# A Mamba layer with an MLP on one core: the two branches of TensorE in the MLP with their bodies swapped

## What is computed

```python
x = x + mixer(layernorm(x))
g = (layernorm(x) @ gate_w.T) * gate_s        # gate_w, up_w: (1408, 512)
u = (layernorm(x) @ up_w.T) * up_s
x = x + ((silu(g) * u) @ down_w.T) * down_s   # down_w: (512, 1408)
```

## Time and profile before

| | us |
|---|---|
| median of 3 runs | 828.86 (828.42 to 829.15) |
| profiled execution | 825.1 |
| its span, first to last instruction | 823.0 |
| TensorE busy | 748.8 (91%) |
| VectorE busy | 512.5 (62%) |
| ScalarE busy | 505.9 (61%) |
| GpSimd busy | 298.0 (36%) |

### The profile page before, as it was taken

One profiled execution on the slowest core, in us unless ns is written; L12 is line 12 of the kernel. 1 busy time (PEld: TensorE's weight loads), 2 busy tenths in 40 slices (PEclk: granted clock), 3 DMA queues, 4 the chain that ended last, 5 costly groups with the idle time before them and its releaser, 6 DMA issues. The chain is left out here.

```text
span 823.0 us, 20282 instructions
## 1 busy us (share of the span) xinstructions
PE 748.8 (91%) x8464; PEld 615.0 (75%) x8464; DVE 512.5 (62%) x839; ACT 505.9 (61%) x963; POOL 298.0 (36%) x245
## 2 busy tenths in 40 slices
PE   5874999999999999999999997548989999999997
PEld 4864778788788788878888884436767887887886
DVE  6883976976976976976976966654622632542331
ACT  6984978978978978888888887024511321331330
POOL 2233366375275276276186175021001001002002
PEclk9986999999999999999999999868999999999999
DMA  9705054443443524423523425921003002102102
GB/s 298 214 2 154 12 117 117 78 112 107 94 98 104 126 66 113 129 68 104 136 66 96 117 66 159 401 59 47 26 16 124 17 5 93 56 0 74 28 1 77
DMA packets 39195, 77.67 MB, mean 94 GB/s; under 512 B 9408, under 2 KB 15040, under 8 KB 39104
## 3 DMA queue, kind: packets, MB, share of 16 engines
q1 hardware_dynamic: 38784, 75.84, 33.4%
q10 hardware_dynamic: 320, 0.52, 0.3%
HBM read 67.43 MB, written 8.92 MB: 93 GB/s over the span
## 5 line engine op out<-in xcount | busy, mean ns | idle before, releaser
L409 POOL TENSOR_TENSOR ring<-tokd,ring 128x1024 f32<-128x1024 f32 x64 | 121.9, 1918 | 198.0 <-ACT tokd L574 127.5
L1064 PE MATMUL ps_proj<-xn_hi,win_hi 128*128 128x256 f32 x608 | 179.2, 295 | 13.9 <-ACT dt_v L506 11.3
L1065 PE MATMUL ps_proj<-xn_lo,win_hi 128*128 128x256 f32 x608 | 172.8, 284 | 0.0
L1066 PE MATMUL ps_proj<-xn_hi,win_lo 128*128 128x256 f32 x608 | 172.4, 284 | 0.0
L1064 PEld LDWEIGHTS ps_proj<-xn_hi,win_hi 128*128 128x128 f32 x608 | 116.7, 192 | 28.2 <-issue 12.9
L1065 PEld LDWEIGHTS ps_proj<-xn_lo,win_hi 128*128 128x128 f32 x608 | 116.9, 192 | 0.3
L1066 PEld LDWEIGHTS ps_proj<-xn_hi,win_lo 128*128 128x128 f32 x608 | 116.8, 192 | 0.0
L799 DVE SCALAR_TENSOR_TENSOR cx<-cin,consts,cx 128x256 f32<-128x256 f32 x240 | 96.3, 477 | 0.0
L1367 POOL TENSOR_TENSOR res<-res,hidden 128x512 f32<-128x512 f32 x16 | 20.5, 1282 | 188.4 <-DVE hidden L1442 188.4
L1399 ACT ACTIVATE silu_g<-pb,scales 128x512 f32<-128x512 f32 x44 | 30.3, 688 | 94.4 <-PE pb L1511 94.3
L1511 PE MATMUL pb<-x1n_hi,wg_hi 128*128 128x512 f32 x176 | 70.4, 400 | 13.0 <-issue 13.0
(11 more groups left out here) (148 smaller groups left out, 1502.9 us busy)
## 6 DMA issues: line engine op xcount, KB each, us to landing
ring<-cum_dram SPq DMA_DIRECT2D x128, 256.0 KB, 4.9
xin<-x SPq DMA_DIRECT2D x8, 512.0 KB, 3.9
res<-x SPq DMA_DIRECT2D x32, 128.0 KB, 2.6
x_in_sb<-x_dram SPq DMA_DIRECT2D x4, 1024.0 KB, 5.8
res<-x_dram SPq DMA_DIRECT2D x16, 256.0 KB, 2.7
out<-res SPq DMA_DIRECT2D x16, 256.0 KB, 2.0
x_dram<-res SPq DMA_DIRECT2D x28, 128.0 KB, 2.4
wg<-gate_w SPq DMA_DIRECT2D x4, 704.0 KB, 9.8
```

What stands on the lines that cost most here:

```text
L409: pool.tensor_tensor(ring[:, g, :, :], own, ring[:, g, :, :], ALU.subtract).then_inc(diffed, 1)
L1064: pe.matmul(out, win_hi[:, k, cols], xn_hi[:, k, :], start=(k == 0), stop=False)
L1065: pe.matmul(out, win_hi[:, k, cols], xn_lo[:, k, :], start=False, stop=False)
L1066: made = pe.matmul(out, win_lo[:, k, cols], xn_hi[:, k, :], start=False, stop=(k == KT - 1))
```

## The change

The two tests are turned from "not zero" to "zero", and the bodies change places. What is executed stays the same matmul for matmul. What changes is which body stands first in TensorE's stream, and so which one is reached without a jump and which one ends in a jump over the other.

```diff
             pe.wait_ge(filled, 1)
             pe.wait_ge(hand.low_any_made, 1)
-            with pe.If(pe.value_load(hand.low_any[:, 0:1].bitcast(I32)) != 0):
+            with pe.If(pe.value_load(hand.low_any[:, 0:1].bitcast(I32)) == 0):
+                gate_up(0, True, True)
+            with pe.Else():
                 gate_up(0, False, True)
-            with pe.Else():
-                gate_up(0, True, True)
             pe.wait_ge(hand.low_any_made, 2)
             pe.wait_ge(down_hi_made, MT)
 
-            with pe.If(pe.value_load(hand.low_any[:, 1:2].bitcast(I32)) != 0):
+            with pe.If(pe.value_load(hand.low_any[:, 1:2].bitcast(I32)) == 0):
+                rest(True)
+            with pe.Else():
                 rest(False)
-            with pe.Else():
-                rest(True)
```

## The result

| | before | changed |
|---|---|---|
| median of the runs beside the prediction, us | 828.64 (4 runs, 825.87 to 829.15) | 816.25 (4 runs, 815.75 to 817.18) |
| profiled execution, us | 825.1 | 815.93 |
| its span, us | 823.0 | 813.8 |
| median of all executions recorded, us | 826.57 (69, 822.24 to 831.07) | 816.41 (19, 814.60 to 819.28) |

The changed kernel is faster by 1.4%, ratio 0.9859 with a 95% interval of 0.9835 to 0.9882. Three later comparisons gave 0.9865 [0.9845, 0.9886], 0.9887 [0.9856, 0.9918] and 0.9887 [0.9866, 0.9908]. In us the four differences of medians are 12.4, 10.4, 9.4 and 9.8. The profiled execution fell by 9.2 us, where I had 9.0. How both can be so is the question of the second half of the experiments.

A forecast was written before the change was run, and what follows sets the result against it. TensorE, busy for 91% of the span, was taken to bound the kernel. The terms 4.0 - 0.3 + 3.4 + 1.9 = 9.0 us gave 816.1 us profiled and a median of 819.8 us, range 818.4 to 823.5.

The forecast's parts named there:

- The stalls are loads of code, and falling through avoids them: Both Ifs: compares of 4125 and 3861 ns wait for code not on the chip; falling through takes near 0.1 us.
- the rival in which the compare costs its four microseconds either way: Both Ifs: the compare stays slow even when falling through, so no difference, 828.9 to 829.2 us; chance 0.06.
- the slower case: End of first body: compares stay slow and the jump waits for the array too, 4.2 us later, 833.1 us; chance 0.04.
- First product: First branch: the first gate and up product starts at 554.3 instead of 558.36, a gain of 4.0 us.
- Slow stretch given back, 0.3 us: After the first branch: TensorE's low clock grant may last longer, costing 0 to 0.6 us extra, taken as 0.3.
- The jump is a full load and hidden by the sequencer's lead: End of first body: the jump loads code for 3.86 to 4.13 us while the array works; gain 3.4 us.
- The rule on taken branches: Skill's rule: taken branches outside two fetched pages load; alone it means the exposed-jump rival, 825.5 us, chance 0.07.
- Clock behind the second branch, 1.9 us: First two down products: 11.86 us against 9.98 in later blocks; with the idling gone, the whole 1.9 us is gained.
- The last jump and the loop cost nothing: Kernel end and loop: a 4.1 us jump hidden by array queue and store, the moved loop stays kept; cost nothing.
- From the profile to the median: Last step: the profile's 9.0 us difference taken off the median of before, 828.86 - 9.0 = 819.8 us.

The follow-up runs named there:

- the cut bodies: Kernel before, its order kept, with the first branch's never executed full-precision body cut to 4 or 7 of 11 tiles: 822.35 and 831.07 us, one execution each.
- a_third: The changed kernel again, unchanged, for a third trace and more timed runs: 816.25 us median (4 runs) beside 825.61 of before.
- a_p4: The changed kernel again, unchanged, for a fourth trace and more timed runs: 817.29 us median (6 runs) beside 827.11 of before.

## Right and wrong, step by step

- *The stalls are loads of code, and falling through avoids them.* Right: 98 and 63 ns for the compares, and the cut bodies show that a taken branch is cheap too when it moves no piece (0.46 us against 4.63). The compares that fall through cost 0.1 us, which refutes the rival in which the compare costs its four microseconds either way, and with it the slower case.
- *First product.* I had it 0.8 us behind the value load's start (554.3 against 553.5); it came after 0.8 (554.57 against 553.8). Gain 4.0 us as forecast, counted from the value load.
- *Slow stretch given back, 0.3 us.* None in this trace (42.60 us against 42.61), 0.3 to 0.4 in the other three of the changed kernel. Right in size.
- *The jump is a full load and hidden by the sequencer's lead.* Right, and shown by exposing it. I charged 3.9 to 4.1 us and in the profile it took 3.35, so it ended before VectorE had low_any, and the array waited 0.03 us, not 0.4. That made the gain 3.8 us, not 3.4. Of the other three traces of the changed kernel one agrees (3.29 and 0.04 us), and in two the jump took 3.7 us and the array waited 0.2 us (a_third, a_p4): the lead of 4.3 us just about covers it.
- *The rule on taken branches.* The jump itself cost 3352 ns, with a piece moved beside it, but the time was not lost, since the array had work queued. The first half is what the Trainium skill states (Runtime: NRT & Kernel Launch, Instruction fetch mechanics: a taken branch to a target outside the fetched pages stalls until that page is loaded), and this trace agrees.
- *Clock behind the second branch, 1.9 us.* 11.86 - 10.22 = 1.6 us in this pair of traces. I had taken the whole difference to later blocks (9.98), and 0.2 us of it isn't the clock's: the changed kernel has the full grant there and still takes 10.22, and without branches it is 10.02. In one of the seven traces of before it is worth 2.9.
- *The last jump and the loop cost nothing.* Right: the jump of 3889 ns ended at 808.9, before the array was done (the drain behind it, 314 ns, ended at 809.2), and the pieces of the loop keep their 40.78 us.
- *From the profile to the median: wrong.* The sum was 4.0 - 0.3 + 3.4 + 1.9 = 9.0. The measured parts from the value load on are 4.03 (558.36 - 554.57 and the 0.24 of the later mixer) + 0.01 + 3.77 + 1.64 = 9.45, less the 0.24: 9.2, and the profile fell by that. The step that failed is the last, "828.86 - 9.0 = 819.8", with the range's low end on the same base. Of the 3.6 us between 819.8 and 816.25, 2.3 are the base: 826.57 is the kernel's usual time, not 828.86. I had allowed only the 0.7 us by which three runs scattered, although the profiled execution, 3.8 us below their median, already said that the scatter was wider. Why the three lay high stays open. Of the other 1.3 us 0.9 are seen in the traces. By their means it is 9.5 us from the value load on, not 9.0 (stalls that cost more in some executions of before count here), and 0.4 for the mixer, which is the draw of seven and four traces. The rest, 0.4 us, is less than these can settle. That the profile came out within 0.2 us is in part luck: single terms were off by 0.3 (slow stretch), 0.4 (wait of the array) and 0.3 us (clock), and the later mixer took 0.24 us back.

## What to carry to other kernels

Where an engine branches on a value, put the body that is nearly always taken directly behind the compare, and look where its closing jump falls: it loaded code too, and was free only because the engine had more work queued ahead than the load took (4.3 us against 3.3 to 3.7). Read the sequencer's own rows by source line for this, since the list of waits put a load of code down to another engine's tile. And when the profiled execution stands 3.8 us from three timed ones, widen the range by that distance, however close the three stand together.

## What the runs showed of the hardware

- A taken branch on TensorE to code that is not loaded costs 3.4 to 4.6 us alone, and 4.7 to 5.1 us when it follows another at once; one over 4 tiles instead of 11, which moved no piece, 0.46 us, a loop's way back over 560 matmuls and loads 0.23 us, one that falls through 0.06 to 0.10 us.
- A jump at the end of a body over one that isn't executed costs 3.3 to 3.9 us of the sequencer. With 4.3 us of matmuls queued it cost the array 0.03 to 0.2 us; with none queued, and with the value load and compare behind it, 4.2 us, and 2.2 more in the down products.
- The clock drop behind 3.4 to 3.8 us of idling cost 1.6 us in five of seven traces of before, and 1.4 and 2.9 in the others (44 down products in 11.61 to 13.12 us against 10.22).
- The same mixer code ended over a range of 3.4 us (553.1 to 556.5) from one execution to the next, and most of that range was there by 90 us (VectorE's L854 started at 87.2 to 91.1).
